# A graph attention layer on one core: VectorE weighs a tile first in its step

## What is computed

```python
xp = (x @ W).reshape(N, H, C)                      # N 3125, H 4, C 256
a_src = einsum('nhc,hc->nh', xp, att_src)
a_dst = einsum('nhc,hc->nh', xp, att_dst)
e = leaky_relu(a_src[src] + a_dst[dst], 0.2)       # one per edge and head
m = segment_max(e, dst)
ee = exp(e - m[dst])
z = segment_sum(ee, dst)
out = relu(segment_sum(xp[src] * (ee / z[dst])[:, :, None], dst) + bias)
```

## Time and profile before

| | |
|---|---|
| runs of the kernel before, median of 3 | 3409.23 us (3398.15 to 3412.22) |
| the profiled execution | 3408.76 us |
| its span in the profile | 3407.0 us |
| mean granted TensorE clock | 0.978 of 2.4 GHz |
| PE busy | 3180.3 us (93%) |
| DVE busy | 2704.7 us (79%) |
| ACT busy | 1187.2 us (35%) |
| POOL busy | 1008.2 us (30%) |
| graph attention, from the first lift to the last evacuation | 1705.2 to 2858.3 us |

### The profile page before, as it was taken

The page is one execution under the profiler, slowest core; times in us unless marked ns, Lnnn a source line. Parts: engine busy times, 40 slices in busy tenths (PEclk is TensorE's granted clock), DMA queues, the critical chain, the costliest instruction groups (busy, mean ns, idle before and its releaser), DMA issues. The chain is left out here.

```text
span 3407.0 us, 43255 instructions
## 1 busy us (share of the span) xinstructions
PE 3180.3 (93%) x14812; PEld 2593.8 (76%) x14812; DVE 2704.7 (79%) x4736; ACT 1187.2 (35%) x1521; POOL 1008.2 (30%) x698
## 2 busy tenths in 40 slices
PE   6899999987999999898879999999999996899998
PEld 5678888866888887676668888887888885777776
DVE  5577776756777777457899999999999875888886
ACT  2011111121111111113265565565566443455444
POOL 1247767657766776640000000000000000000000
PEclk8999999998999999999999999999999998999999
DMA  7933323344444445435554453453454223222221
GB/s 253 373 84 71 56 55 72 55 124 79 89 86 90 90 85 128 89 88 152 149 139 122 119 148 86 124 156 99 115 149 117 68 54 105 73 78 72 80 82 43
DMA packets 286025, 366.08 MB, mean 107 GB/s; under 512 B 190330, under 2 KB 190430, under 8 KB 285910
## 3 DMA queue, kind: packets, MB, share of 16 engines
q1 hardware_dynamic: 95828, 282.24, 28.1%
q0 software_dynamic: 184656, 65.68, 11.0%
q10 hardware_dynamic: 5426, 16.70, 1.4%
HBM read 272.64 MB, written 90.80 MB: 107 GB/s over the span
## 5 line engine op out<-in xcount | busy, mean ns | idle before, releaser
L1421 PE MATMUL G_acc<-values,whole_plain 125*125 125x257 f32 x5000 | 1104.9, 383 | 47.6 <-DVE whole_plain L1381 30.0
L1421 PEld LDWEIGHTS G_acc<-values,whole_plain 125*125 125x125 f32 x5000 | 937.7, 189 | 204.6 <-DVE whole_plain L1381 39.7
L331 POOL DMA_INDIRECT counts<-E_twins_now,E_cells_now x400 | 868.4, 2171 | 388.0 <-issue 256.1
L1285 ACT ACTIVATE whole_plain<-whole_plain,G_asrc_slope 125x750 f32<-125x750 f32 (+1 forms) x400 | 377.8, 946 | 418.0 <-DVE whole_plain L1368 417.3
L1368 DVE SCALAR_TENSOR_TENSOR whole_plain<-whole_plain,G_asrc_most 125x750 f32<-125x750 f32 (+1 forms) x400 | 411.3, 1028 | 45.3 <-PE G_acc L1421 44.9
L952 DVE SCALAR_TENSOR_TENSOR N_least<-xT_plain,asrc_all,N_least 125x750 f32<-125x750 bf16 (+1 forms) x336 | 339.1, 1014 | 0.0
L1259 POOL DMA_DIRECT2D gat<-xT_plain x100 | 53.4, 535 | 955.9 <-ACT xT_plain L1301 955.9
L228 PE MATMUL V_v_ps<-whole,xT_space 128*125 128x512 f32 x1200 | 293.2, 402 | 34.7 <-DVE xT_space L256 23.2
L228 PEld LDWEIGHTS V_v_ps<-whole,xT_space 128*125 128x125 f32 x1200 | 221.6, 188 | 106.0 <-DVE xT_space L256 42.1
L228 PE MATMUL Q_q_ps<-whole,xT_space 128*125 128x512 f32 x1200 | 288.0, 399 | 14.0 <-DVE xT_space L256 14.0
L228 PE MATMUL K_v_ps<-K_wv,xT_space 128*125 128x512 f32 x1200 | 293.4, 401 | 0.0
(11 more groups left out here) (183 smaller groups left out, 3517.0 us busy)
## 6 DMA issues: line engine op xcount, KB each, us to landing
whole_plain<-counts SPq DMA_DIRECT2D x222, 328.1 KB
counts<-K_zeros POOLq DMA_DIRECT2D x50, 763.5 KB, 8.6
xT_whole<-xnT SPq DMA_DIRECT2D x75, 500.0 KB
whole_plain<-counts SPq DMA_DIRECT2D x74, 382.8 KB
xnT<-xT_whole SPq DMA_DIRECT2D x25, 500.0 KB
gat<-xT_plain POOLq DMA_DIRECT2D x100, 125.0 KB, 2.3
E_row<-edge_keys ACTq DMA_DIRECT2D x25, 488.3 KB
E_row<-edge_keys SPq DMA_DIRECT2D x25, 488.3 KB
```

Of the source, the lines that this page charges most:

```text
L331: nc.gpsimd.indirect_dma_start(out=counts_cells, out_offset=bass.IndirectOffsetOnAxis(ap=self.cells_now[:, slot, c:c + 1], axis=0), in_=se ...
L1285: nc.scalar.activation(here, here, ACT.Exp, bias=asrc_slope[:, u % H, j:j + 1]).then_inc(exp_ready, 1)
L1421: m = nc.tensor.matmul(acc[0:T, t, 0:CW], weight[:, k % RING, t * T:(t + 1) * T], values[:, j, u % H, :], start=(j == 0), stop=(j == NT - 1))
```

## The change

In each step DVE's three pieces change their order. Nothing is added or removed, and ACT, PE, POOL and SP keep their programs.

```diff
             for k in range(STEPS):
                 u, j = k // NT, k % NT
+                if k + WEIGH_AHEAD < STEPS:
+                    weigh(k + WEIGH_AHEAD)
                 if k + AHEAD < STEPS:
                     lift(k + AHEAD)
                 for m in range(least_by(k), least_by(k + 1)):
                     nearest.step(dve, absent, m)
-                if k + WEIGH_AHEAD < STEPS:
-                    weigh(k + WEIGH_AHEAD)
                 for v in range(1, UN):
                     if k == fold_at(v) + 2:
                         nearest.floors(dve, tr, v, 0)
```

## The result

The changed kernel takes 3529.44 us (median of 4 runs, 3525.98 to 3532.98), where the kernel before, on the same chip, takes 3407.97. The ratio is 1.0361, with a 95% interval of 1.0336 to 1.0386: 121 us slower. The forecast was 3520 and 3482 to 3556. The profiled execution of after took 3530.6 us, with a span of 3528.8.

The account below looks back on a forecast made before the run. DVE bounds the first 20 steps, DVE and PE the middle, PE the end; afterwards DVE's longer wait path sets the pace. Weigh starts plus floors, evacuations and late counts gave +111 on the stage, so 3520 us, range 3482 to 3556.

Parts of the forecast that it names:

- The order of limits: Graph attention: DVE full in the first 20 steps, DVE and PE in the middle, PE once the leasts are over.
- The first regime: First 20 steps, two leasts each: weigh waits for leasts, mask and exponential; step 4.10 to 6.25 us, +37.
- The ring: Later steps: weigh, lift, exponential, weigh sets the step, 3.20 us at 875 columns, 2.83 at 750.
- Floors and shifts: Two per unit, behind the least; they fill the new gap before they cost; together 15 us.
- Evacuations: On ACT at unit boundaries, ahead of mask and exponential; overrun 0.4 us, with a keep 1.1: +4, bounds 0 and 15.
- Late counts: Three stretches of keeps where ACT waits for transfers beside the broadcast: 5 us each, +15, bounds 9 and 35.
- The end: End of the graph attention: PE ends at 2969, where today it ends within a microsecond of 2858; difference +111.
- What would show it: Profile after: DVE's exponential waits over 100 us, in nearly every step; steps 6.25, then 2.83; no PE waits at the end.
- PE's clock: First 20 steps: at 1.2 GHz PE's step takes 6.0 us, under 6.25, so costs only if the level stays down.
- the rival at 3535: PE's clock falls in the first 20 steps and stays down at 3.20 us steps, some 15 us; 5 in 100.
- The rival of equal counts: Whole kernel: equal instruction count and ample ACT time mean no difference, 3409; 3 in 100.

Follow-up runs that it names:

- e2_lead_only: The kernel before with the new order (weigh, lift, least) in the first 20 steps alone, the old order from step 20 on: 3449.21 us, ratio 1.0109.
- e7_end_only: The kernel before with the new order only from step 330 on, where no leasts are left: 3419.98 us, ratio 1.0044.
- e3_exp_first: The changed kernel with ACT taking a step's exponential ahead of its keeps and masks: 3510.64 us, ratio 1.0307.
- e5_narrow_rows: The changed kernel with POOL broadcasting only the first 64 columns of the rows of shifts from unit 2 on: 3513.23 us, ratio 1.0315.

## Why the prediction was right

*The order of limits* was right: DVE's loss is passed on in full (e2_lead_only), and DVE's idle time at the end covers nothing (e7_end_only).

*The first regime*: forecast a step of 6.25 and +37 us, measured 6.26, and weigh(22) 128.5 us after weigh(0) for 91.2, +37.3. The link through the mask is shown by e3_exp_first.

*The ring*: forecast 3.20 and 2.83, measured 3.20 and 2.84. The 0.01 makes 3 us over 299 steps. The lifts and weighs ahead of step 0, which had the new order already, told the length at 875 columns before the change was made. Over the step of before, the ring costs 0.16 us in the middle, 0.24 at the end, and 0.14 to 0.27 at 875 columns, where steps of before were 3.06, 2.93 and, from weigh(58) on, 3.03 us, and not 2.94 throughout as the prediction had it. Its sum goes by the new steps, so this moved nothing in it.

*Floors and shifts*: forecast 15, measured 15 (steps of 3.52 and 4.07 at 875 columns, 3.27 and 3.68 at 750).

*Evacuations*: forecast 4, measured 5 (0.4 at units with a mask, 1.1 to 1.4 with a keep as well).

*Late counts*: forecast 15 within 9 and 35, measured 24 (the steps' excess over ring and floors: 5.3 at weigh 95, 5.6 and 0.8 at 195 and 196, 2.6 and 2.6 at 296 and 297, and seven of 0.3 to 1.8). This is the mis-sized term. Some 17 of the 24 came through ACT, which is what the prediction had counted. The counts were not later than before: ACT waited 37.9 us for them then and 29.7 after. But more of it arrived: at weigh(96) ACT stood 7.10 us and DVE felt 5.23 of it. The rest, some 6.5, the prediction had put at nothing: three weighs, from steps 147, 247 and 297, waited for their own staged counts, and the lift of step 249 for its rows of shifts, the 4.9 and 1.6 us of the list above. The prediction says that a weigh frees its slot up to a step earlier, "which I count at nothing", and not that it also wants its own counts earlier. That this is why they were late is likely and not shown: e2_lead_only has one such wait, 2.2 us, in a step with the old order.

*The end*: the forecast compared PE's end, weigh(399) + 3.7, with 2858, which is the end of the last evacuation. Measured, that end comes 6.0 us behind weigh(399) (2972.52 + 2.55 - 2969.11), so the comparison was 2.3 us short.

Summed: 111 + 3 + 1 + 9 + 2 is 126 for the stage's 125.6. The difference to the 121.8 of the spans is what the unchanged stages varied by, 8.8 us less ahead of it and 5.0 more behind it, and was not to be forecast. So the 9 us between forecast and time are less than the 15 by which the stage was under-counted, and that is luck, not foresight.

*What would show it*: DVE's waits rose over 100 (140.6), and the waits for PE vanished. "In nearly every step" was wrong for the list, which has 166 of them for 400: in the middle they are too short to be listed. It was right for the steps.

*PE's clock.* The forecast said that a lower clock in the first regime would cost nothing while it lasts. Three stretches of after, in the columns of the earlier trace rows:

```profile
1725.00:1775.00 50.00, 33.48 (x117) 25.05 (x116) 35.09 (x39) 20.45 (x22) 0.00 (x0) 0.86 0.33 87
...
1755.00:1761.00 6.00, 5.71 (x13) 4.49 (x14) 3.93 (x5) 2.55 (x3) 0.00 (x0) 0.50 0.00 0
...
1772.00:1792.00 20.00, 10.70 (x46) 8.00 (x44) 12.86 (x13) 8.84 (x11) 1.04 (x2) 1.00 0.35 91
```

The granted clock was 0.86 on the mean of the first, where the kernel before had 1.00 from 1715 to 1811. It went back and forth between the levels: 0.50, which is 1.2 GHz, at 1755 to 1761, full at 1772 to 1792, and 0.50 again at 1793 to 1799. Before the fall at 1755 PE had stood 2.96 us in each of two steps in a row, at 1742.78 and 1749.04, waiting for the weigh. The steps stayed 6.26 throughout, since the products of a step still fit in at the low level: 13 of 14 recorded took 5.71 us. It was at 0.51 once more at 1840 to 1846, when the steps were 3.20 already, and they stayed 3.20; the level did not stay down, which was the condition of the rival at 3535. The Trainium skill, page "TensorE: Matmul & The Clock Gate", section "HAM oscillation — how this bites in real kernels", tells of a loop whose repeated gaps bring the clock down again and again. The trace agrees, with falls in some of the steps and not in each; the price did not arise, since PE was not the bound.

*The rival of equal counts.* The Trainium skill, page "VectorE: DVE Perf Modes", section "Rules for kernel authors", says of chained DVE operations to keep down their count and not the semaphores. Read as "equal counts, equal time", as the rival read it, it does not carry over to this case: the count is the same 4736 on DVE and the time 3.6% longer. What DVE waits for here is the semaphore of another engine, ACT.

## What to carry to other kernels

Before reordering an in-order engine that hands work to another and takes it back, write down the ring (hand over, other engine's time, take back) and compare its length with the step: what stands between the two hands is what covers it, and idle time elsewhere on either engine does not. Look behind the other engine's queue as well: here one of its waits, the mask's for the least, stood ahead of the needed result and cost 2.16 us a step (6.26 for 4.10), against 0.14 to 0.27 for the ring alone. And measure steps from start to start, since a loss of 0.16 us in each of 230 steps is in no list of waits.

## What was not expected of the hardware

A load of counts beside a broadcast of 732 KB was waited for 7.10 us, and beside one of 62.5 KB, in e5_narrow_rows, 2.97. And how much of a late transfer reaches the bound depends on the slack behind it, more than on how late it is: in the profiled executions 6.59 us of waiting on ACT, and 1.44 behind it, cost DVE 2.04 and 0.97 before; 7.10 cost it 5.23 after.
